# Block 0 of a four-block network: scores and maxima in pieces of 32 array columns

## The reference

```python
def _attn(q, k, v, mask):
    scores = jnp.einsum('bqhd,bkhd->bhqk', q, k) / np.float32(np.sqrt(HD))
    scores = jnp.where(mask[:, None, None, :], jnp.float32(-jnp.inf), scores)
    w = jax.nn.softmax(scores, axis=-1)
    return jnp.einsum('bhqk,bkhd->bqhd', w, v)
# x (16, 56, 128), ctx (16, 1500, 128): for each of 6 layers
# q from the normed x, k and v from ctx with that layer's weights, rope on q and k
```

## Time and profile before

| | us |
|---|---|
| median of 3 runs | 6555.9 (6546.36 to 6572.31) |
| the profiled execution's own time | 6555.0 |
| its span, first to last instruction | 6553.2 |
| PE busy, of the span | 6048.2 (92%) |
| DVE busy | 3934.0 (60%) |
| ACT busy | 3319.4 (51%) |
| POOL busy | 2241.2 (34%) |

### The profile page before, as it was taken

How to read it: one execution, slowest core, us unless ns; L and a number is a source line. 1 busy time by engine, 2 the same in 40 slices (tenths; PEclk the granted TensorE clock), 3 DMA queues, 4 the chain that set the end, 5 groups by cost and what they waited for, 6 DMA issues and landing times.

```text
span 6553.2 us, 141305 instructions
## 1 busy us (share of the span) xinstructions
PE 6048.2 (92%) x56229; PEld 4426.8 (68%) x56229; DVE 3934.0 (60%) x8724; ACT 3319.4 (51%) x6401; POOL 2241.2 (34%) x2180
## 2 busy tenths in 40 slices
PE   5899899998999989999989999999789999989998
PEld 4666576665766657666653777777557777756983
DVE  3777777777777777777765334444544444444553
ACT  1565666656566565666653334444333333333763
POOL 4555555555555555555520000000001111146440
PEclk8899999999999999999989899999889999999998
DMA  2665656756566565675750010000100000021000
GB/s 58 103 112 86 102 95 100 107 94 105 92 101 110 91 102 96 102 110 90 112 97 1 18 37 31 29 29 29 26 15 10 15 15 11 15 86 33 1 2 22
DMA packets 396488, 407.90 MB, mean 62 GB/s; under 512 B 125575, under 2 KB 372946, under 8 KB 393786
## 3 DMA queue, kind: packets, MB, share of 16 engines
q1 hardware_dynamic: 395834, 398.85, 34.4%
HBM read 158.00 MB, written 0.46 MB: 24 GB/s over the span
## 4 chain that ended last, share of the span: by engine, by line
PE 69%; DVE 9%; POOL 8%; issue 6%; ACT 4%; DMA 2%; POOLq 1%; SPq 1%; DVEq 0%; ACTq 0%
PE psum L2224 10%; PE psum L2191 9%; PE psum L1554 6%; PE psum L1542 6%; PE psum L1528 6%; PE psum L2235 4%; PE psum L1568 4%; PE psum L1576 3%; POOL slot_context L3410 3%; PE psum L1674 2%; DVE row_max L1898 2%; PE psum L434 2%; PE psum L420 2%; PE psum L1683 1%; POOLq L3417 1%
## 5 line engine op out<-in xcount | busy, mean ns | idle before, releaser
L1898 DVE TENSOR_REDUCE row_max<-psum 112x1 f32<-112x500 f32 x2304 | 1442.0, 668 | 274.1 <-PE psum L1542 269.4
L2019 ACT ACTIVATE weights<-psum 125x448 f32<-125x448 f32 x2304 | 1152.5, 544 | 734.0 <-PE psum L1528 718.6
L1528 PEld LDWEIGHTS psum<-query_stack,key_stack 121*125 121x125 bf16 x9216 | 838.4, 140 | 360.9 <-issue 163.9
L1542 PE MATMUL psum<-key_stack,query_stack 97*112 97x500 bf16 x2304 | 904.8, 393 | 103.3 <-DVE row_max L1898 80.3
L1528 PE MATMUL psum<-query_stack,key_stack 121*125 121x112 bf16 x9216 | 921.2, 223 | 72.8 <-ACT weights L2019 65.0
L2775 POOL TENSOR_TENSOR l_ctx_v<-l_ctx_v,l_ctx_w 125x512 f32<-125x512 f32 x48 | 60.8, 1268 | 2186.2 <-DVE l_ctx_v L2769 2186.2
L2224 PE MATMUL psum<-l_ctx_v,l_turned 125*128 125x128 f32 x5376 | 713.7, 281 | 15.9 <-ACT l_turned L2260 12.2
L2302 DVE TENSOR_REDUCE l_stat<-psum 128x1 f32<-128x1500 f32 (+1 forms) x224 | 391.6, 1748 | 543.6 <-PE psum L2191 543.6
L2224 PEld LDWEIGHTS psum<-l_ctx_v,l_turned 125*128 125x128 f32 x5376 | 643.1, 191 | 49.4 <-ACT l_turned L2260 39.7
L1554 PE MATMUL psum<-weights,values 125*17 125x112 f32 x18432 | 674.9, 265 | 0.2 <-ACT weights L2019 0.2
L1554 PEld LDWEIGHTS psum<-weights,values 125*17 125x17 f32 x18432 | 378.0, 97 | 260.6 <-ACT weights L2019 138.7
(11 more groups left out here) (537 smaller groups left out, 10262.5 us busy)
## 6 DMA issues: line engine op xcount, KB each, us to landing
key_stack<-key_parts SPq DMA_DIRECT2D x1728, 125.0 KB, 4.5
ctx_t<-in_ctxT SPq DMA_DIRECT2D x96, 750.0 KB
l_ctx_v<-in_ctxV SPq DMA_DIRECT2D x32, 750.0 KB
query_stack<-query_parts SPq DMA_DIRECT2D x576, 28.0 KB, 3.6
l_ctx_t<-in_ctxT SPq DMA_DIRECT2D x16, 750.0 KB
slot_context<-in_ctxV SPq DMA_DIRECT2D x16, 750.0 KB
key_stack<-ctx_mask_rows SPq DMA_DIRECT2D x576, 3.9 KB
sm_w<-in_sm_w SPq DMA_DIRECT2D x3, 2048.0 KB
```

The source lines that it names most:

```text
L1528: mm = e.matmul(self.k.psum[0:KN, h, (p % 4) * QC:(p % 4 + 1) * QC], ks[:, p, kt * KN:(kt + 1) * KN], q[:, p * QC:(p + 1) * QC])
L1542: e.matmul(self.k.psum[0:QC, 2 + n % 2, 0:500], q[0:ROWS_MAX, p * QC:(p + 1) * QC], ks[0:ROWS_MAX, p, c * 500:(c + 1) * 500]).then_inc(sel ...
L1898: e.tensor_reduce(self.largest[:, i % PAIRS, i // PAIRS:i // PAIRS + 1], k.psum[0:QC, 2 + i % 2, 0:500], AX.X, ALU.max, negate=True).then_ ...
L2019: e.activation(half(self.p[kt % 2], h), self.k.psum[0:KN, h, 0:HALF], ACT.Exp).then_inc(self.exped.sem, 1)
```

## The change

A new helper, `quarters`, cuts a product into pieces of at most 32 stationary columns. Each piece is a weight load and a matmul of its own, reads the same moving operand again, and writes its own 32 partitions of the result. The scores (125 columns: 32, 32, 32, 29) and the maxima (112 columns: 32, 32, 32, 16) are made by it. Waits stand at the first piece and the signal at the last one. Weighing and side products are as they were.

```diff
+def quarters(e, out, lhsT, rhs, **kw):
+
+    m = lhsT.shape[1]
+    for lo in range(0, m, 32):
+        hi = min(lo + 32, m)
+        mm = e.matmul(out[lo:hi], lhsT[:, lo:hi], rhs, **kw)
+    return mm
...
         for p in range(4 * h, 4 * h + 4):
-            mm = e.matmul(self.k.psum[0:KN, h, (p % 4) * QC:(p % 4 + 1) * QC], ks[:, p, kt * KN:(kt + 1) * KN],
+            mm = quarters(e, self.k.psum[0:KN, h, (p % 4) * QC:(p % 4 + 1) * QC], ks[:, p, kt * KN:(kt + 1) * KN],
                           q[:, p * QC:(p + 1) * QC])
         mm.then_inc(self.scored.sem, 1)
...
-        e.matmul(self.k.psum[0:QC, 2 + n % 2, 0:500], q[0:ROWS_MAX, p * QC:(p + 1) * QC],
+        quarters(e, self.k.psum[0:QC, 2 + n % 2, 0:500], q[0:ROWS_MAX, p * QC:(p + 1) * QC],
                  ks[0:ROWS_MAX, p, c * 500:(c + 1) * 500]).then_inc(self.max_scored.sem, 1)
```

## The result

| | us |
|---|---|
| median of the changed kernel, 4 runs | 6609.15 (6601.65 to 6611.47) |
| median of the kernel before beside it, 4 runs | 6555.08 (6546.36 to 6572.31) |
| ratio, 95% interval | 1.0071 [1.0049, 1.0094] |
| the profiled execution's own time and span | 6601.65, 6599.8 |

The change makes the kernel 0.7% slower, about 50 us. The forecast of 6480 was wrong in its sign. 6609 lies in the given range of 6425 to 6680, but by luck: the upper end stood there for loads that go in turn, and that did not happen.

What follows compares the result with a forecast made beforehand. TensorE, 93% busy in block 0, was taken as the bound, VectorE next at 75%. Direct rounds (43 us) and score pace (65, reduced to 43), times 0.85, gave 73; some 75 off 6555.0 made 6480 us, range 6425 to 6680.

Steps and rivals of the forecast that it cites:

- (a): Rounds with side products: scores pay about 0.09 us more, the weighing saves its 0.09; net nothing.
- (b): Rounds without side products: both shape changes go, 0.25 us in each of 174 rounds, 43 us saved.
- The 0.05 for the exposed load: Scores after a weighing: 0.05 us extra because their first 125-column load had nothing to hide behind.
- (c): Score products: four pieces take 49 ns instead of 56, a half 0.20 us instead of 0.225; 65 us saved.
- (d): Maxima in pieces: each stays at 0.21 to 0.22 us; 0 us gained.
- What it adds: TensorE: 34,560 more load and matmul pairs, 60% more instructions, bounded at 49 to 100 ns per four; 49 taken.
- What is late next: VectorE and query DMAs take back gains: 65 us becomes 43, then 43 + 43 times 0.85 leaves 73 us.
- A price per piece: Rival: pairs fed no faster than 24 to 25 ns, 100 ns per four pieces; about 6900 us, chance 0.10.
- Absorbed: Rival: VectorE, reads of maxima and query DMAs take back most; 20 us remain, 6535 us, chance 0.18.
- Loads in turn: Rival: four 32-column loads queue for one path, 75 ns per four instead of 56; about 6670 us, chance 0.08.
- one after another: Rival: bf16 pieces run serially, a half 0.9 us and a maximum 0.86; 9500 us, chance 0.04.
- The signs announced: Changed profile: weighing before scores 0.40 us, half 0.20, VectorE about 77%, maxima and query waits up some tens of us.

Runs made afterwards that it cites:

- light kernels: The kernel before and the changed kernel, each with the copies into the key stack cut to a sixteenth: 6555.64 and 6526.02 us.
- direct version: Against the kernel before, scores and maxima in pieces only in rounds whose scores follow a weighing directly: 6539.94 against 6558.21 us, ratio 0.9971.
- short reductions: Both kernels with key copies cut to a sixteenth, and VectorE's maximum reading 250 of 500 columns: 6465.83 before, 6422.03 us changed, ratio 0.9932.
- light change: The change measured between the two kernels with key copies cut to a sixteenth: 6526.02 against 6555.64 us, ratio 0.9955.
- the version with every even round: Against the kernel before, pieces in rounds whose scores follow a weighing directly and in every even round: 6534.0 against 6556.22 us, ratio 0.9955.
- e2_split2: The kernel before with each weighing product cut in two along its moving columns, scores and maxima whole: 6570.17 us, ratio 1.0018.
- e4_scores_only: Against the kernel before, only the scores in pieces and the maxima whole: 6855.36 us, ratio 1.0456.

## Why the prediction was wrong

The account is made between the first and the last weighing of block 0, from TensorE's records: 3188.6 us before, 3220.3 after, 32 more. Of the 47 us that the spans differ by, the other 15 lie outside; that remainder was anywhere between 3365 and 3382 in the twelve profiles, though the program is the same there, so it is scatter from one execution to the next.

| from start to start, undisturbed | before, ns | after, ns | us, all |
|---|---|---|---|
| half of the scores to a maximum, 2272 | 222 | 197 | -57 |
| maximum to weighing, 1136 | 306 | 215 | -103 |
| weighing to scores, 218 | 508 | 384 | -27 |
| weighing to a side product, 932 | 508 | 487 | -20 |
| side product to scores, 932 | | + 92 | +86 |
| sum | | | -121 |

(Undisturbed is the value that 15% of the cases lie below; between scores and weighing some records are missing.)

**(a) Side-product rounds, net nothing.** Right: 92 ns more before scores, 91 less before the weighing. A saving that I had not seen came with it, 21 ns in the weighing before a side product.

**(b) Direct rounds.** The sizes are right: 0.09 + 0.12 us, against 0.09 + 0.11. The 0.05 for the exposed load came too: the half behind a weighing went from 275 to 199 ns.

**(c) The scores' pace.** Right: 49 ns per product, 0.197 us a half, 57 us before anything is lost again; the forecast had 65. The 25 ns of the row are those of the halves behind a maximum (222 to 197). Behind a side product it was 16 (223 to 207) and behind a weighing 76, with the exposed load in it; taken so, the row would be 59. **(d)** Right.

Undiminished, (b) and (c) were 119 us by the forecast. The trace has 121 for everything, and 20 of these are the weighing before a side product, which the forecast didn't have: that the two sums meet so closely is in part luck. So the products themselves did what was forecast, and the time went elsewhere: 121 less in the products and yet 32 more between the weighings are 153 us of new standstill. Two steps failed.

**"What it adds" failed, and this turned the sign.** The step priced 34,560 pairs of load and matmul by the array's pace and by how fast a pair can follow a pair. Both bounds, 49 and 100 ns per four, were about the single piece, and the supply of the instructions themselves stood at nothing, without a reason. The price lies in the packet of 256: with the pieces it lasts 5.7 us in the mean, and behind the copies of keys the next one isn't always there by then. The pile-up grew by 102 us; the cut of the copies gives 83 back (68 between the weighings of the profiled executions).

The page "Runtime: NRT & Kernel Launch" of the Trainium skill, section "Instruction fetch mechanics", says that an engine gets its instructions in blocks of 16 KiB, 256 instructions each, over a DMA queue of its own, and that this is mostly hidden because instructions are issued more slowly than they are fetched. The trace agrees on the block (16.4 KB a packet, 255 places from stop to stop). It disagrees on "hidden": stops of up to 2.1 us here, and 83 us that went with other engines' copies.

**"What is late next" was too small.** It took 46 us off the 119. In the light kernels, where the supply hardly counts, the pieces save 34 us between the weighings (3186.3 to 3152.1), so 87 of 121 come back as standstill. The direct version points the same way: 19 us by the medians where 43 were forecast. The waits for the maxima and the queries were named; those for the keys (0.9 to 13.7 us) and the side products' norms (L1659, 20.9 to 29.3 us between the light kernels) were not. The share was seven tenths and not four. With the short reductions 80 of 121 still come back. Which wait takes how much is open: I can name only the lines that grew, and apart from the reading of the maxima no run changes one of them by itself. That the chain of keys and queries over the other engines has its own rhythm, and TensorE meets it somewhere else when it is faster, is a guess.

**The rivals.** "A price per piece" had the right suspicion, the feeding of pairs, and the wrong mechanism: no piece is slower (49 ns per four, under the 61 from which it decided), so its 6900 is far off. "Absorbed" names most of what happened to the gain, and would have been nearly right without the supply (the light change is worth 30 us; it said 20). "Loads in turn" and "one after another" are excluded by the 0.20 us of a half.
The page "TensorE: Matmul & The Clock Gate" of the Trainium skill, section "Wait — 56ns, not 53.3ns?", has a floor of about 25 ns from start to start, on which "A price per piece" leaned. The changed kernel's rows have 16 pieces in 0.20 us, 12 ns each over whole halves, so for pieces in four different strips the trace disagrees with it.

**The signs announced.** The weighing between pieces was announced at 0.40 and came at 0.38, the half at 0.20 and came at 0.197, VectorE's share was to rise to 77% and stayed at 75 (2452.71 of 3270, and 2453.29 before), the clock stayed at 0.97, and the waits for the maxima and the queries grew by 28 us together, as announced. I had listed four ways to be wrong, and none was a stop inside a group, the one that came.

## What to carry to other kernels

When a change multiplies instructions, divide: how many microseconds will 256 instructions of that engine last? Where that comes to some 5 us while the DMA engines are busy for half of the time or more with other things, as here (5.7 us, 60%), expect stops in the middle of groups ("issue" in the waits, at equal distances in instructions); spread the dense rounds between others, as the version with every even round does, or take only those with the best return. These are the values of this one kernel; no run looked for the border between them. And a saving of tens of nanoseconds per round on a leading engine with 7% of idle time was worth about a third of its arithmetic here (34 of 121 us in the light kernels).

## What the hardware showed that I had not expected

- Four bf16 pieces of 32 columns in four strips cost 49 ns together, the same as the moving operand's time, over thousands of groups.
- With 28 moving columns the weighing's sixteen groups take 0.65 us. Less the 0.11 of the way back that is 34 ns per group of four, where a quarter of the 112 columns' 100 ns would be 25: some 8 ns per pair is the fastest stream seen here. With 56 moving columns (e2_split2) a group took 51 ns, half of the 100. So my reading is that somewhere between 56 and 28 columns a piece begins to cost by its number; no run lies between.
- A change of shape costs 0.09 to 0.13 us also between bf16 products, each way (e4_scores_only: 0.31 for 0.22, 0.35 for 0.22).
- The same DMA traffic that costs nothing in one kernel (6555.64 against 6556.22 without and with it) costs 83 us in another, by way of the instructions: the waits on the copied keys themselves are 13.7 us with it and 15.1 without.
